# Wider copies out of PSUM in the maxima stage of a gated cross-attention block: three banks an instruction, every fourth group split 7 to 1, without loops

## What is computed

```python
q = (query @ Wq + bq).reshape(Bq, Sq, H, DK)
k = (key @ Wk + bk).reshape(Bq, Sk, H, DK)
v = (value @ Wv + bv).reshape(Bq, Sk, H, DK)
scores = jnp.einsum('bqhd,bkhd->hbqk', q, k) / np.sqrt(DK)
attn = jax.nn.softmax(scores.reshape(H * Bq, Sq, Sk), axis=0).reshape(H, Bq, Sq, Sk)
out = jnp.einsum('hbqk,bkhd->bqhd', attn, v).reshape(Bq, Sq, H * DK)
...
x = x + jnp.tanh(g_xattn[0]) * attention(layernorm(x), ctx_1024)
x = x + jnp.tanh(g_ffn[0]) * ffn(layernorm(x))
```

## Time and profile before

| | us |
|---|---|
| median of 3 runs | 974.15 (967.47 to 976.32) |
| the profiled execution | 967.42, of which 965.1 lie between its first and last instruction |
| `maxima`, first matmul to end of the fold | 170.8 to 354.9 |
| mean granted TensorE clock | 0.94 |

### The profile page before, as it was taken

How to read it: one execution, slowest core, us unless ns; L and a number is a source line. 1 busy time by engine, 2 the same in 40 slices (tenths; PEclk the granted TensorE clock), 3 DMA queues, 4 the chain that set the end, 5 groups by cost and what they waited for, 6 DMA issues and landing times. The chain is left out here.

```text
span 965.1 us, 21136 instructions
## 1 busy us (share of the span) xinstructions
PE 779.0 (81%) x8056; PEld 433.1 (45%) x8056; DVE 840.1 (87%) x1036; ACT 739.4 (77%) x1117; POOL 490.7 (51%) x338
## 2 busy tenths in 40 slices
PE   3698892777777767999999999999999887088576
PEld 1455551211111124666656665666566576033133
DVE  6769952799999978999999999999999969868668
ACT  3255562899999979899999999999999604479593
POOL 4122231000000001999999999999999965134400
PEclk9898896899999979999999999999999989589869
DMA  9489798545555657569665976678575652000013
GB/s 291 151 261 340 260 325 313 190 176 194 198 205 183 222 192 199 164 184 321 174 197 167 297 214 172 195 252 257 156 214 166 222 180 87 1 1 0 1 48 128
DMA packets 112393, 180.91 MB, mean 187 GB/s; under 512 B 10032, under 2 KB 37296, under 8 KB 112304
## 3 DMA queue, kind: packets, MB, share of 16 engines
q1 hardware_dynamic: 112304, 179.67, 58.0%
HBM read 137.70 MB, written 41.94 MB: 186 GB/s over the span
## 5 line engine op out<-in xcount | busy, mean ns | idle before, releaser
L816 POOL TENSOR_TENSOR e<-e,recip 128x768 f32<-128x768 f32 (+3 forms) x256 | 387.3, 1557 | 37.9 <-DVE recip L858 37.9
L782 ACT ACTIVATE e<-ps_att 128x512 f32<-128x512 f32 x512 | 301.1, 647 | 28.5 <-PE ps_att L720 27.1
L847 DVE TENSOR_REDUCE pair_sums<-e 128x128 f32<-128x2048 f32 x128 | 292.6, 2286 | 16.5 <-ACT e L782 16.5
L720 PE MATMUL ps_att<-arena 128*128 128x128 bf16 x2048 | 194.1, 220 | 4.6 <-ACT ps_att L790 4.5
L553 ACT ACTIVATE copies<-ps_max 128x1024 bf16<-128x1024 f32 x192 | 179.1, 1027 | 20.5 <-PE ps_max L533 20.5
L533 PE MATMUL ps_max<-q_head,k_head 128*128 128x512 bf16 x512 | 138.4, 386 | 60.5 <-DVE high L572 21.8
L735 PE MATMUL acc<-e,arena 128*32 128x128 f32 x4096 | 178.8, 293 | 6.6 <-DVE e L828 3.9
L720 PEld LDWEIGHTS ps_att<-arena 128*128 128x128 bf16 x2048 | 150.2, 98 | 64.4 <-ACT e L782 4.8
L716 PE MATMUL ps_att<-shift,minus 128*128 128x512 bf16 x384 | 149.5, 389 | 7.5 <-POOL zero_w L807 6.2
L735 PEld LDWEIGHTS acc<-e,arena 128*32 128x32 f32 x4096 | 106.2, 110 | 36.5 <-POOL e L816 8.1
L577 DVE TENSOR_TENSOR high<-copies,high 128x3072 bf16<-128x3072 bf16 x64 | 112.0, 1751 | 0.0
(11 more groups left out here) (128 smaller groups left out, 852.7 us busy)
## 6 DMA issues: line engine op xcount, KB each, us to landing
arena<-k_stack SPq DMA_DIRECT2D x256, 256.0 KB, 3.0
k_stack<-parts SPq DMA_DIRECT2D x64, 256.0 KB, 3.9
q_stack<-parts SPq DMA_DIRECT2D x64, 256.0 KB, 3.7
k_head<-k_stack SPq DMA_DIRECT2D x16, 1024.0 KB, 5.6
q_head<-q_stack SPq DMA_DIRECT2D x16, 1024.0 KB, 7.8
arena<-q_stack SPq DMA_DIRECT2D x64, 256.0 KB, 4.8
arena<-in_x_dram SPq DMA_DIRECT2D x5, 1024.0 KB, 7.9
arena<-in_ctx_dram SPq DMA_DIRECT2D x4, 1024.0 KB, 6.8
```

The costliest lines, as they stand in the source:

```text
L720: last = nc.tensor.matmul(bank[:, j * P:(j + 1) * P], ks[:, i % KRING, b * P:(b + 1) * P], qs[:, h, b * P:(b + 1) * P], start=False, stop= ...
L782: nc.scalar.activation(e_at(qc * STEPS + i, half * HB, (half + 1) * HB).rearrange("p q b i -> p b q i"), ps[(qc * (2 * STEPS) + 2 * i + ha ...
L816: nc.gpsimd.tensor_tensor(part, part, by_pairs(recip[:, kc % 2, :], share), ALU.mult).then_inc(pool_scaled, 1)
L847: nc.vector.tensor_reduce(pair_sums[:, :, h // 2, :], e[:, g % RING // 2].rearrange("p q s b i -> p q i (s b)"), AX.X, ALU.add).then_inc(s ...
```

## The change

The banks are counted one by one (8 to a group) instead of as four chunks of two. A group's banks are now divided into three sections with a semaphore each:

- front: banks 0 to 2 (SPAN = 3);
- back: banks 3 to 5, or 3 to 6 in each fourth group (`copied_banks(g)` is 6, and 7 where g % 4 is 3);
- rest: what is left, banks 6 and 7, or bank 7 alone.

ACT copies front in one instruction and back in one (L571): 1536 elements a partition each, 2048 for a back of four banks. DVE takes rest straight from PSUM (L586) and merges 6 or 7 banks (L595). PE fills front, rest, back in that order, and in the group after one with seven copied banks front, back, rest. The loops are gone: all 64 groups are written out, with constants in the waits. SP's loads wait for all three sections of the last group of head h-2. The fold at the end is the same.

```diff
-    COPIED = NC - 1
+    BANKS = NC * LANES
+    SPAN = 3
+    SEVEN_EVERY = 4
+    def copied_banks(g):
+        return 2 * SPAN + (g % SEVEN_EVERY == SEVEN_EVERY - 1)
...
             def _(pe):
-                    for u in range(UNITS):
-                        bp, kc = u // NC, u % NC
-                        if not (first and bp == 0):
-                            g = (r * 2 + i) * GROUPS + bp
-                            if kc == COPIED:
-                                pe.wait_ge(updated, g * 2 - 1)
-                            else:
-                                pe.wait_ge(copied, g * COPIED + (kc + 1 - COPIED))
...
+                def front(g):
+                    if g:
+                        pe.wait_ge(copied, 2 * g - 1)
+                    banks(g, 0, SPAN, front_scored)
+                def back(g):
+                    if g:
+                        pe.wait_ge(copied, 2 * g)
+                        if copied_banks(g) > copied_banks(g - 1):
+                            pe.wait_ge(direct, g)
+                    banks(g, SPAN, copied_banks(g), back_scored)
+                def rest(g):
+                    if g:
+                        pe.wait_ge(direct, g)
+                        if copied_banks(g) < copied_banks(g - 1):
+                            pe.wait_ge(copied, 2 * g)
+                    banks(g, copied_banks(g), BANKS, rest_scored)
+                for g in range(H * GROUPS):
...
+                    front(g)
+                    if g and copied_banks(g) < copied_banks(g - 1):
+                        back(g)
+                        rest(g)
+                    else:
+                        rest(g)
+                        back(g)
             def _(act):
-                        if not (first and bp < RING):
-                            act.wait_ge(updated, (g - RING) * 2 + 2)
-                        for kc in range(COPIED):
-                            act.wait_ge(scored, g * NC + (kc + 1))
-                            nc.scalar.activation(copies[:, bp % RING, kc, :], ps[:, kc, :], ACT.Copy).then_inc(copied, 1)
+                for g in range(H * GROUPS):
+                    if g >= RING:
+                        act.wait_ge(updated, g - RING + 1)
+                    for first, end, done in ((0, SPAN, front_scored), (SPAN, copied_banks(g), back_scored)):
+                        act.wait_ge(done, g + 1)
+                        nc.scalar.activation(copies[:, g % RING, first:end], ps[:, first:end], ACT.Copy
+                                             ).then_inc(copied, 1)
             def _(dve):
...
+                def straight(g):
+                    dve.wait_ge(rest_scored, g + 1)
+                    if g:
+                        dve.wait_ge(direct, g)
+                        if copied_banks(g) < copied_banks(g - 1):
+                            dve.wait_ge(updated, g)
+                    at = slice(copied_banks(g), BANKS)
+                    nc.vector.tensor_tensor(high[:, at], ps[:, at], high[:, at], ALU.max).then_inc(direct, 1)
+                def merge(g):
+                    dve.wait_ge(copied, 2 * g + 2)
+                    if g:
+                        dve.wait_ge(updated, g)
+                        if copied_banks(g) > copied_banks(g - 1):
+                            dve.wait_ge(direct, g)
+                    at = slice(0, copied_banks(g))
+                    nc.vector.tensor_tensor(high[:, at], copies[:, g % RING, at], high[:, at], ALU.max
+                                            ).then_inc(updated, 1)
```

More of the change, by code:

```diff
@@ L503, in _ @@
                     sp.dma_start(q_head[:, i], q_stack[:, i].rearrange("c p x -> p c x")).then_inc(loaded[i], 16)
[L504 to L511, removed]
+                for h in range(2, H):
+                    for done in (front_scored, back_scored, rest_scored):
+                        sp.wait_ge(done, (h - 1) * GROUPS)
+                    sp.dma_start(k_head[:, h % 2], k_stack[:, h].rearrange("c p x -> p c x")).then_inc(loaded[h % 2], 16)
+                    sp.dma_start(q_head[:, h % 2], q_stack[:, h].rearrange("c p x -> p c x")).then_inc(loaded[h % 2], 16)
                 for h in range(H):
@@ L537, in _, with banks @@
[L537 to L541, removed]
+                def banks(g, first, end, done):
+                    h, bp = g // GROUPS, g % GROUPS
+                    for u in range(first, end):
+                        kc, b = u // LANES, bp * LANES + u % LANES
+                        last = nc.tensor.matmul(
+                            ps[:, u, :], k_head[:, h % 2][:, kc, b * P:(b + 1) * P],
+                            q_head[:, h % 2].rearrange("p c (b q) -> p c b q", q=P)[:, :, b, :], start=True, stop=True)
+                    last.then_inc(done, 1)
@@ L543, in _ @@
+                for g in range(H * GROUPS):
+                    h, bp = g // GROUPS, g % GROUPS
+                    if bp == 0:
+                        pe.wait_ge(loaded[h % 2], (h // 2 + 1) * 32)
+                    front(g)
[5 more added lines that the diff above has]
+                        back(g)
             @block.scalar
             def _(act):
-                def head(r, i, first):
-                    for bp in range(GROUPS):
-                        g = (r * 2 + i) * GROUPS + bp
-                        if not (first and bp < RING):
-                            act.wait_ge(updated, (g - RING) * 2 + 2)
-                        for kc in range(COPIED):
-                            act.wait_ge(scored, g * NC + (kc + 1))
-                            nc.scalar.activation(copies[:, bp % RING, kc, :], ps[:, kc, :], ACT.Copy).then_inc(copied, 1)
@@ L588, in store_sums @@
+                for g in range(H * GROUPS):
+                    straight(g)
+                    merge(g)
+                dve.wait_ge(updated, H * GROUPS)
+                dve.wait_ge(direct, H * GROUPS)
+                both = high[:].rearrange("p (c j) x -> p c j x", j=LANES)
+                nc.vector.tensor_tensor(shift[:], both[:, :, 0], both[:, :, 1], ALU.max).then_inc(folded, 1)
 def store_sums(sp, rows_out, out_s, stored, some=range(B)):
```

20 lines of the change are left out of this document (6 added, 14 removed).

## The result

The changed kernel takes 985.97 us (median of 4 runs, 983.99 to 990.58), the kernel before 970.81 us on the same footing (4 runs, 965.17 to 976.32). The measured ratio is 1.0217, with a 95% interval of 1.0182 to 1.0253; it isn't the quotient of these two medians, which is 1.0156. Before's four runs scatter by 11 us, so their median says little. In the later measurements before's medians are 964.7, 965.0 and 965.7 us (19, 13 and 17 runs), and 985.97 is 2.1 to 2.2% above them. So the change is slower beyond the noise, but whether by more or less than 2% is open. The forecast was 988, from 974 to 1006, slower. For the profiled execution the forecast comes to a span of 965.1 + 17 = 982.1; it is 983.5.

What follows compares the result with a forecast made beforehand. DVE was taken as the bound at 2.80 us a group. Sixteen rounds at +1.05 us gave +17: 984.4 from the profiled time, 991 from the median; the forecast was 988, between the two, range 974 to 1006.

Steps and rivals of the forecast that it cites:

- What bounds the kernel: In `maxima`, DVE runs without a pause at 2.80 us a group; ACT has 0.08 us of slack a group.
- The new instructions: Work on ACT and DVE over four groups: ACT from 10.86 to 11.07 us, DVE from 11.20 to 10.94.
- The chain: Handoffs between PE, ACT and DVE in `maxima`: a round of four groups takes 12.25 us against 11.20.
- straight update 3: DVE's direct PSUM update in a round's third group, at 7.77 us; 4.48 us from it to the merge of seven.
- the walk: Stepping one round of four `maxima` groups through PE, ACT and DVE by handoffs: 12.25 us, +17 us over sixteen rounds.
- Group 2: Second group of a round: its merge comes at 6.10 us where DVE alone would be at 5.98, losing 0.12.
- Straight update 1 waits for this merge itself: DVE at a round's start: the direct update waits for the seven-bank merge to end, 2.05 us, costing 0.12 a round.
- What costs nothing: Written-out code, removed loop work and head loads change nothing; `attend` and `ffn` stay untouched, so the loss passes on whole.
- The engines evening out: Rival, chance 0.13: in `maxima` the long path fits behind DVE's work; -2 to +9 us, 965 to 983.
- only the order on PE: Part of the likeliest case: one-bank update and four-bank copy cost nothing, two groups lose 0.12 each; +4 us, 971 to 978.
- The clock's fall: Rival, chance 0.12: TensorE's clock drops to 0.50 in `maxima`; +40 to +50 us if it lasts, 1008 to 1024.
- the other footing: Whole-kernel base time: the median of three runs, 974.15 us, as against the profiled execution's 967.4.

Runs made afterwards that it cites:

- the wide copies with back ahead of rest: Against the kernel before: loops written out, three banks a copy, always six copied banks, back filled before rest; `maxima` 184.3 us, ratio 1.0008.
- the last kernel: Against the separately copied seventh bank, filled last: only every eighth group copies seven, and straight updates get own running-maximum places; `maxima` 183.2 us, ratio 0.9978 to before.
- the split seventh bank: Against the changed kernel: back always before rest, and the seventh bank copied by its own instruction and filled last; `maxima` 184.7 us, ratio 1.0021 to before.
- the kernel with wide copies alone: Against the kernel before: loops written out, three banks a copy, always six copied banks, rest filled before back; `maxima` 188.1 us.
- the kernel with the order alone: Against the changed kernel: back filled before rest in every group, seven copied banks kept in each fourth group; `maxima` 198.4 us.
- The kernel with two and four banks: Against the kernel before: loops written out, always six copied banks in copies of two and four, rest filled last; `maxima` 197.3 us.
- rest ahead of both: Against the kernel before: loops written out, three banks a copy, always six copied banks, PE fills rest before front and back; `maxima` 234.6 us.

## Why the prediction held, and where it was off

**What bounds the kernel.** DVE at 2.80 us a group with ACT close behind. Confirmed by the wide copies with back ahead of rest: ACT's work fell from 10.85 to 10.65 a round (8 copies at 1.331) and nothing moved. In the last kernel DVE's work fell, and the round fell with it.

**The new instructions.** Three banks 1.452 and four 1.877 us (1.45 and 1.88 forecast), a merge of seven 2.026 (2.015), a straight update of one bank 0.684 (0.695). The changed kernel's rows from 170 to 372 us, shapes kept apart; the last merge lies behind that stretch:

```profile
L571 ACT ACTIVATE copies<-ps_max 128x1536 bf16<-128x1536 f32 x112 | 155.4, 1452 | 34.7 <-PE ps_max L528 34.5
L595 DVE TENSOR_TENSOR high<-copies,high 128x3584 bf16<-128x3584 bf16 x15 | 30.4, 2026 | 14.7 <-ACT copies L571 14.7
L571 ACT ACTIVATE copies<-ps_max 128x2048 bf16<-128x2048 f32 x16 | 30.0, 1877 | 2.0
L586 DVE TENSOR_TENSOR high<-ps_max,high 128x512 bf16<-128x512 f32 x16 | 10.9, 684 | 0.0
```

**The chain.** From straight update 3 to the merge of seven the walk had 4.48; the timeline has 224.57 - 220.09 = 4.48. Group 2 lost 0.13 (0.12 forecast), group 3 nothing, as forecast. ACT stood idle before the back copies of groups 2, 3 and 4 by 0.87, 0.12 and 0.24 us (distances between starts less 1.33), where some 0.8, 0.1 and 0.2 were forecast. The wait before the merge of seven was forecast as 1.07 and is 1.08 by distances (224.57 - 222.89 - 0.60); the row's 0.99 counts from the end of the short update's tail.

**The term that was mis-sized.** The prediction's "Straight update 1 waits for this merge itself: 2.015 + 0.04 = 2.05" takes 2.16. I had taken the 0.04 from the fold, which waits for one thing of its own engine. The straight update waits for three counts, and its wait on the merge is an instruction of its own ahead of it: the merge ends at 226.59, that wait at 226.68, the update starts at 226.73. Its price is 0.13, not 0.04, and that is 0.10 of the 0.115 by which a round is longer than the 12.25 of the walk; the rest is the merge's 0.01. Everything behind it in the round is late by just this: the walk's 7.77, 8.90 and 10.57 are 7.89, 9.02 and 10.68 in the timeline. Sixteen rounds: 18.7 instead of 17.

**What costs nothing.** The written-out code: shown (11.200, 0.9988). The head loads: no wait of PE for a DMA in the steady stretch. The parts behind: busy times within 0.5%, 3 us less, not more.

**The rivals.** The engines evening out did not occur; the split seventh bank shows that it would have needed short pieces behind DVE's update, and then +0.6 us is what comes of it. The lower bound, only the order on PE, is the kernel with wide copies alone: +4.0 for the +4 forecast. The clock's fall did not occur in the changed kernel. That rival's price was also added up wrongly: 13.5 and 14.4 us a round are +37 and +51 us, which is 1004 to 1019 from the profiled time; 1024 mixes in the other footing.

**Breaking up the copy.** In the kernel before, DVE and ACT were full. In the kernel with the order alone they are busy 145.03 and 147.32 of 158 us, and splitting the long copy there gained 13.7 us. The sentence of the Trainium skill on breaking up instructions (Perfetto Trace Analysis, Optimizing Scalar/DVE Operations) is about engines that aren't saturated, a condition that the prediction doesn't name. With it the trace agrees.

**The number.** That 988 came within 2 us of 986 is partly luck. It was made of two footings, and before's fourth run, 965.2, and the later 49 runs show that 974 was a high median; from 965 the same sum gives 982, four too low. On the ratio, 17 of 967 was 1.76%, and 2.17% was measured, with 1.82% at the interval's low end; the span's is 1.91%. Of the gap to the ratio, some 1.5 us are the self-wait and 0.2 the longer merge. The rest I don't attribute. The runs of about 975 us that several kernels show, before among them, come from behind `maxima`, as far as one profile tells: for the seventh bank as a copy of its own the profiled execution took 975.9 us, and what follows its fold took 617.4 us, where the eleven other profiles have 606.3 to 610.2.

**A cause that was not separated.** In the seven-bank group three things lengthen the path: DVE's bank in front, four matmuls in place of three, and the copy of 1.88 in place of 1.45. The split takes all three away together. By the distances, the last two are worth 0.22 + 0.43. The kernel with two and four banks shows these two at a cost (0.21 a group) without the first, but beside a shorter other copy.

## What to carry to other kernels

Where a buffer isn't doubled, and an engine queue serves two consumers, look at which of their refills stands behind which: a section that waits for consumer A holds up everything for consumer B behind it, and busy time will not show it until B's piece is long. Walk the path through all engines for one period with start-to-start distances and the measured handoffs, before believing a balance of sums: here the sums said -2 us and the walk said +17. When work is moved in small amounts, give the moved part an instruction of its own and fill it last, so that the rest doesn't wait with it; here that was worth 13.7 us.

## What the runs showed of the hardware

A wait for an earlier instruction of the same engine isn't one price. It is 0.03 us from end to start where the waiting instruction carries it (the fold behind the last merge), and 0.13 where a separate wait instruction stands ahead (224.57 + 2.03 to 226.73 in the changed kernel): 0.04 until that one starts, its own 0.05, and 0.04 more until the update starts. Without any wait on the instruction just ahead, DVE starts the next one 0.08 before the end of the one before it (1.94 behind a merge of 2.02).

The clock: matmuls of 512 columns in bursts, over eight banks in turn, kept 1.00 from 182 to 340 us in nine of the ten experiments and in the changed kernel. In the changed kernel PE was busy 103.55 of the 158 us (66%, where the walk had 66%), with pauses up to 1.3 us; with the order alone the pauses reached 1.6 us, and with two and four banks PE was busy 99.92 us. The exception is rest ahead of both. These are its windows, and last, out of order, one in which a head's loads run at full clock (columns as in the earlier trace rows):

```profile
189.30:192.70 3.40, 3.27 (x10) 0.88 (x8) 1.83 (x3) 2.79 (x2) 0.00 (x0) 0.51 1.05 376
192.80:261.00 68.20, 36.12 (x154) 13.39 (x153) 55.55 (x39) 53.05 (x38) 0.00 (x0) 1.00 0.38 134
261.00:264.40 3.40, 2.87 (x9) 0.79 (x7) 2.23 (x3) 2.79 (x2) 0.00 (x0) 0.50 1.05 399
346.40:349.80 3.40, 3.39 (x9) 1.03 (x8) 2.77 (x2) 1.76 (x2) 0.00 (x0) 0.50 0.95 357
390.70:394.10 3.40, 3.25 (x9) 0.93 (x8) 1.85 (x3) 2.79 (x2) 0.00 (x0) 0.51 1.04 381
203.60:207.00 3.40, 1.86 (x10) 0.66 (x9) 2.60 (x3) 2.79 (x2) 0.00 (x0) 1.00 1.05 398
```

With PE busy 36 of 68 us and pauses up to 2.2 us, the clock fell to 0.5 four times in the stage for 3.4 us each and came back. All four falls stand where the DMA engines are full (share 0.95 to 1.05), but most heads' loads, like the one in the last row, pass at 1.00; whether the loads have a part in the falls, no run shows. So the swings between the two levels that the Trainium skill describes (TensorE: Matmul & The Clock Gate, A second HAM failure mode: psum-queue depth-cycling) do exist in this stage, in the one kernel whose PE is idle longest at a time; in the changed kernel, which cycles through the banks as well, they did not occur.
